# Cross attention in a six-stage layer: score matmuls as pairs of float32r tiles of 64 rows, small work cut into single matmuls at fixed steps

## What is computed

```python
q = x @ Wq;  k, v = split(ctx @ Wkv)            # heads of 16 channels
q, k = apply_axial_rope(q, pos), apply_axial_rope(k, pos)
p = softmax(q @ k.T / sqrt(16))                 # 512 x 512 for each head
y = (p @ v) @ Wout + bout
x = layernorm(x + y)
```

## Time and profile before

| | us |
|---|---|
| median of 3 runs | 3314.42 (3313.26 to 3315.32) |
| the profiled execution | 3316.54 |
| its span, first to last instruction | 3314.8 |
| TensorE busy in the span | 2716.1 (82%) |
| VectorE busy | 1958.6 (59%) |
| ScalarE busy | 1433.1 (43%) |
| GpSimd busy | 1177.7 (36%) |
| mean granted TensorE clock | 0.900 |
| exponentials of the cross attention, first to last unit | 2490.0 to 3117.5 |

### The profile page before, as it was taken

The page is one execution under the profiler, slowest core; times in us unless marked ns, Lnnn a source line. Parts: engine busy times, 40 slices in busy tenths (PEclk is TensorE's granted clock), DMA queues, the critical chain, the costliest instruction groups (busy, mean ns, idle before and its releaser), DMA issues.

```text
span 3314.8 us, 50665 instructions
## 1 busy us (share of the span) xinstructions
PE 2716.1 (82%) x20138; PEld 1454.0 (44%) x20154; DVE 1958.6 (59%) x3064; ACT 1433.1 (43%) x2577; POOL 1177.7 (36%) x1118
## 2 busy tenths in 40 slices
PE   5788888876677676589988898888768989899787
PEld 3565656553223232268845444444433333333244
DVE  3323232333689889956526566656655657476477
ACT  3232333320545555423426262635315546465555
POOL 0443333441566666600023625243243424241000
PEclk8888888887888888799998999998879989899999
DMA  2222222130330304032332424243155435252301
GB/s 87 71 59 62 52 78 60 47 87 14 121 116 13 127 26 140 13 140 95 137 108 86 128 90 125 93 122 130 39 117 107 105 69 112 61 109 53 118 26 39
DMA packets 209370, 280.04 MB, mean 84 GB/s; under 512 B 84640, under 2 KB 111680, under 8 KB 208240
## 3 DMA queue, kind: packets, MB, share of 16 engines
q1 hardware_dynamic: 209136, 276.81, 29.4%
HBM read 192.08 MB, written 59.12 MB: 76 GB/s over the span
## 4 chain that ended last, share of the span: by engine, by line
PE 39%; DVE 10%; issue 5%; ACT 4%; POOL 2%; DMA 1%; SPq 0%; ACTq 0%; DVEq 0%; POOLq 0%
PE ps L236 7%; PE ps L3368 4%; PE ps L1846 4%; PE ps L1857 4%; PE ps L3355 4%; PE ps L3341 3%; PE ps L3300 3%; PE ps L3332 2%; PE ps L2512 1%; ACT arena L3446 1%; PE ps L2520 1%; DVE arena L2775 1%; DVE arena L1434 1%; DMA arena<-arena 1%; DVE arena L2773 1%
## 5 line engine op out<-in xcount | busy, mean ns | idle before, releaser
L236 PE MATMUL ps<-arena 128*128 128x512 f32 (+3 forms) x1280 | 473.6, 522 | 18.3 <-ACT arena L2612 6.1
L3545 DVE TENSOR_REDUCE arena<-ps 128x1 f32<-128x512 f32 x512 | 330.3, 685 | 229.2 <-PE ps L3341 227.8
L3446 ACT ACTIVATE arena<-ps 128x512 f32<-128x512 f32 x512 | 287.8, 597 | 283.2 <-PE ps L3355 279.7
L1466 POOL TENSOR_TENSOR arena<-arena 128x1024 f32<-128x1024 f32 x128 | 311.0, 2430 | 192.9 <-DVE arena L1458 192.9
L1482 PE MATMUL ps<-arena 128*128 128x512 f32 x512 | 267.2, 662 | 55.8 <-POOL arena L1466 55.5
L1458 DVE TENSOR_TENSOR_SCAN arena<-ps,arena 128x1024 f32<-128x1024 f32 x128 | 291.5, 2278 | 32.9 <-ACT ps L1449 32.9
L236 PEld LDWEIGHTS ps<-arena 128*128 128x128 f32 (+2 forms) x1296 | 193.2, 154 | 252.3 <-issue 172.9
L1449 ACT ACTIVATE ps<-arena 128x511 f32<-128x511 f32 x256 | 165.1, 679 | 188.3 <-DVE arena L1458 188.1
L576 POOL TENSOR_TENSOR arena<-arena 128x31 f32<-128x31 f32 (+15 forms) x217 | 130.1, 600 | 324.2 <-DMA arena<-d_a 307.8
L3355 PE MATMUL ps<-arena 99*128 99x512 bf16 x512 | 198.4, 390 | 45.3 <-ACT arena L3446 33.4
L3341 PE MATMUL ps<-arena 96*128 96x512 bf16 x512 | 201.4, 395 | 19.1 <-issue 15.4
(11 more groups left out here) (352 smaller groups left out, 5254.1 us busy)
## 6 DMA issues: line engine op xcount, KB each, us to landing
arena<-d_bc SPq DMA_DIRECT2D x32, 1024.0 KB, 5.7
arena<-d_x SPq DMA_DIRECT2D x24, 1024.0 KB, 6.8
arena<-d_parts SPq DMA_DIRECT2D x192, 128.0 KB, 4.6
d_x<-arena SPq DMA_DIRECT2D x64, 256.0 KB, 2.5
arena<-arena SPq DMA_DIRECT2D x128, 128.0 KB, 2.1
arena<-in_D_wlm SPq DMA_DIRECT2D x12, 1024.0 KB, 6.6
d_parts<-arena SPq DMA_DIRECT2D x32, 384.0 KB, 2.4
d_signs<-arena SPq DMA_DIRECT2D x32, 256.0 KB, 2.1
```

The costliest lines, as they stand in the source:

```text
L236: ins = pe.e.matmul(ps[:m, :n], lhsT(k), rhs(k), start=(k == 0), stop=(k == chunks - 1))
L1466: pool.e.tensor_tensor(h, h, s.bc[:, turn % s.SLOTS, 1], ALU.mult).then_inc(*pool.up("scan_hC"))
L3446: act.e.activation(s.E[:, k % 2, j], s.rexp.bank((u, i)), ACT.Exp).then_inc(*s.rexp.empty(act, (u, i)))
L3545: dve.e.tensor_reduce(s.mx[:, u % 2, t, h:h + 1], s.rmax.bank((u, m)), AX.X, ALU.max, negate=True).then_inc(*s.rmax.empty(dve, (u, m)))
```

## The change

- **Scores.** q and k are split into two float32r parts (hi, lo) instead of three bf16 ones. Three products of parts give 48 rows, and two rows of ones against the two parts of the negated maximum make 50. Head 2h stands in rows 0 to 49 and head 2h+1 in rows 64 to 113, so two heads' score matmuls use the two halves of the array. A step now has two score tiles of each kind; there are 16 steps (`PAIRS`) in an iteration.
- **Small work.** `small` replaces `misc`. It gives each matmul (or group of transposes) of an item a step of its own: Rq at 3, 3, 5, 5, Rk at 7, 7, V at 9, 9 (four matmuls each time), a y tile at 11, 11, 13, 13. The y tiles of a batch spread over the next three iterations. ang and the xT stay in iterations with i a multiple of 4, at steps 11 to 15.
- **Banks.** 3 for exponential scores, 3 for maximum scores, 1 for values, 1 for small work.
- **Buffers.** `aT` has two copies. The residual of odd batches uses the buffer of x. Bias sums, residual loads, square root, scaling and stores move by some steps.
- **Queues.** A row copy is 2 transfers instead of 3; a stack stays at 6. SP first writes two rows of ones for each half. The maxima are transposed in fp32 instead of bf16.

```diff
-    Q_PARTS = (0, 1, 0, 2, 1, 0)
-    K_PARTS = (0, 0, 1, 0, 1, 2)
-    N = 6 * 16
+    Q_PARTS = (0, 0, 1)
+    K_PARTS = (0, 1, 0)
+    N = 3 * 16
     UNITS, HU = 4 * B, 8
     G = 4
     KEYS = L // P
     STEPS = HU * T
+    PAIRS = STEPS // 2
+    RESIDUAL_AT = (4, 8, 12, 13)
...
-        s.Qs, s.Ks = carve(s.SLOTS, s.HU, L, dt=BF16), carve(s.SLOTS, s.HU, L, dt=BF16)
+        s.Qs, s.Ks = carve(s.SLOTS, s.HU // 2, L, dt=F32R), carve(s.SLOTS, s.HU // 2, L, dt=F32R)
...
-        s.ring = Ring("cross", ps, 6, 2, [(name, s.EMPTIES[name[0]]) for i in s.iterations() for _, name in s.misc(i)])
-        s.rexp = Ring("cross_exp", ps, 0, 2, [((u, e), "act") for u in range(s.UNITS) for e in range(s.STEPS)])
-        s.rmax = Ring("cross_max", ps, 2, 3, [((u, m), "dve") for u in range(s.UNITS) for m in range(s.STEPS)])
-        s.rav = Ring("cross_av", ps, 5, 1, [((u, g), "act") for u in range(s.UNITS) for g in range(2)])
+        s.rexp = Ring("cross_exp", ps, 0, 3, [((u, e), "act") for u in range(s.UNITS) for e in range(s.STEPS)])
+        s.rmax = Ring("cross_max", ps, 3, 3, [((u, m), "dve") for u in range(s.UNITS) for m in range(s.STEPS)])
+        s.rav = Ring("cross_av", ps, 6, 1, [((u, g), "act") for u in range(s.UNITS) for g in range(2)])
+        s.misc = [item for i in s.iterations() for item in s.small(i)]
+        s.ring = Ring("cross", ps, 7, 1, [(name, s.EMPTIES[name[0]]) for name, _ in s.misc])
...
+    def small(self, i):
+
+        s = self
+        f, nb, b = i + s.AHEAD, (i + s.AHEAD + 1) // C, i // C - 1
         starts = (i + s.AHEAD + 1) % C == 0 and nb < B
+        items = []
+        if s.unit(i) is not None:
+            items.append((("mT", i, 1), [1]))
+        if s.unit(i - 1) is not None:
+            items.append((("turn", i - 1, 1), [2]))
         if s.unit(f) is not None and i != -1:
-            yield 1, ("Rq", f)
+            items.append((("Rq", f), [3, 3, 5, 5]))
+        if s.unit(i - 1) is not None:
+            items.append((("aT", i - 1), [6]))
+        if s.unit(f) is not None and i != -1:
+            items.append((("Rk", f), [7, 7]))
+        if s.unit(i + 1) is not None:
+            items.append((("mT", i + 1, 0), [8]))
+        if s.unit(f) is not None:
+            items.append((("V", f), [9, 9]))
         if s.unit(i) is not None:
-            yield 3, ("mT", i, 1)
-        if s.unit(i - 1) is not None:
-            yield 5, ("turn", i - 1, 1)
-        if s.unit(f) is not None and i != -1:
-            yield 7, ("Rk", f)
-        if s.unit(i - 1) is not None:
-            yield 11, ("aT", i - 1)
-        if s.unit(f) is not None:
-            yield 15, ("V", f)
-        ends = s.unit(i - 1) is not None and i % C == 0
+            items.append((("turn", i, 0), [10]))
+        if i == -2:
+            items += [(("Rq", f + 1), [11, 11, 13, 13]), (("Rk", f + 1), [15, 15])]
         if starts:
-            yield 17, ("ang", nb)
-        if s.unit(i + 1) is not None:
-            yield 19, ("mT", i + 1, 0)
-        if s.unit(i) is not None:
-            yield 21, ("turn", i, 0)
-        if i == -2:
-            yield 25, ("Rq", f + 1)
-            yield 27, ("Rk", f + 1)
-        for t in range(T):
-            if ends:
-                yield 22 + 2 * t, ("y", i // C - 1, t)
-            if starts:
-                yield 23 + 2 * t, ("xT", nb, t)
-
-
+            items += [(("ang", nb), [11])] + [(("xT", nb, t), [12 + t]) for t in range(T)]
+        if i == s.UNITS:
+            items += [(("y", b, t), [7 + 2 * t] * C) for t in range(T)]
+        elif b >= 0 and i % C:
+            items.append((("y", b, (0, 0, 2, 3)[i % C]), [11, 11, 13, 13]))
+            if i % C == 1:
+                items.append((("y", b, 1), [14, 15, 15, 16]))
+        return [(name, [s.PAIRS * i + at for at in steps]) for name, steps in items]
+
+    def pieces(self, step):
+
+        return [(name, k, len(steps)) for name, steps in self.misc for k, at in enumerate(steps) if at == step]
+
+    def ended(self, step):
+
+        return [name for name, steps in self.misc if steps[-1] == step]
+
+    def res(self, b):
+
+        return (self.xr, self.x)[b % 2]
...
-        for a in range(3):
-            sp.e.dma_start(s.Qs[96 + a:97 + a, u % s.SLOTS, s.G * half:s.G * (half + 1)],
-                           s.mT[s.G * a:s.G * (a + 1), half, :]).then_inc(*sp.up(f"cross_max_rows{half}", 16))
+        for p in range(2):
+            at = 64 * p + s.N
+            sp.e.dma_start(s.Qs[at:at + 2, u % s.SLOTS, 2 * half:2 * half + 2].bitcast(F32),
+                           s.mT[4 * p:4 * p + 4, half, :].bitcast(F32)).then_inc(*sp.up(f"cross_max_rows{half}", 16))
...
-            sp.e.dma_start(dst[16 * a:16 * a + 16], d[:, :, part, :].rearrange("h d l -> d h l")).then_inc(*sp.up(f"cross_stack_{'qk'[w]}", 16))
+            for p in range(2):
+                at = 64 * p + 16 * a
+                sp.e.dma_start(dst[at:at + 16].bitcast(F32), d[p::2, :, part, :].rearrange("h d l -> d h l")).then_inc(*sp.up(f"cross_stack_{'qk'[w]}", 16))
...
+    def sp_one_rows(self, sp):
+
+        s = self
+        sp.e.wait_ge(*sp.at_all("cross_ones"))
+        for p in range(2):
+            at = 64 * p + s.N
+            sp.e.dma_start(s.Ks[at:at + 2].rearrange("p a h l -> p (a h) l").bitcast(F32), spread(s.one[:2], 1, s.SLOTS * s.HU // 2)).then_inc(*sp.up("cross_one_rows", 16))
...
-            if i >= 0 and i % C == 0 and nb < B:
+            if i % C == 0 and nb < B:
                 s.sp_x(sp, nb)
+            if s.unit(i) is not None:
+                s.sp_rows(sp, i, 1)
+            if i % C == 0 and i >= 2 * C:
+                s.sp_store(sp, i // C - 2)
             if s.unit(f) is not None:
                 s.sp_swap(sp, f, 0)
-            if s.unit(i) is not None:
-                s.sp_rows(sp, i, 1)
-            if s.unit(f) is not None:
                 s.sp_swap(sp, f, 1)
-            if i % C == 1 and i > C:
-                s.sp_store(sp, i // C - 1)
-            if s.unit(f) is not None:
                 s.sp_stack(sp, f, 0)
             if s.unit(i + 1) is not None:
                 s.sp_rows(sp, i + 1, 0)
             if s.unit(f) is not None:
                 s.sp_stack(sp, f, 1)
-            if i >= 0 and i % C == 0 and nb < B:
+            if i % C == 0 and nb < B:
                 s.sp_ctx(sp, nb)
-            if i > 0 and i % C == 2:
-                s.sp_residual(sp, i // C)
+            if i in s.RESIDUAL_AT:
+                s.sp_residual(sp, s.RESIDUAL_AT.index(i))
...
-        hi, mid, lo = (s.parts[:, w, a] for a in range(3))
+        hi, lo = (s.parts[:, w, a] for a in range(2))
         e.tensor_copy(hi, s.m1[:, w]).then_inc(*eng.up_step("cross"))
         eng.e.wait_ge(*eng.at_step("cross"))
-        e.tensor_tensor(s.rest[:, w], s.m1[:, w], hi, ALU.subtract).then_inc(*eng.up_step("cross"))
-        eng.e.wait_ge(*eng.at_step("cross"))
-        e.tensor_copy(mid, s.rest[:, w]).then_inc(*eng.up_step("cross"))
-        eng.e.wait_ge(*eng.at_step("cross"))
-        e.tensor_tensor(lo, s.rest[:, w], mid, ALU.subtract).then_inc(*eng.up(f"cross_parts_{n}"))
+        e.tensor_tensor(lo, s.m1[:, w], hi.bitcast(F32), ALU.subtract).then_inc(*eng.up(f"cross_parts_{n}"))
...
+            ins = e.matmul(ps, wt[:, piece, cols], src[:, piece, :], start=(piece == 0), stop=(piece == pieces - 1))
...
+            for t in (2 * piece, 2 * piece + 1):
...
-                ins = e.transpose(ps.bitcast(BF16)[:3 * s.G, t * P:(t + 1) * P], s.mp[:, half, t].rearrange("p a h -> p (a h)"), s.identb)
+                ins = e.transpose(ps[:2 * s.G, t * P:(t + 1) * P], s.mp[:, name[2], t].rearrange("q p a h -> q (p a h)").bitcast(F32), s.ident)
...
-        s, slot, h, t = self, u % self.SLOTS, m // T, m % T
+        s, slot = self, u % self.SLOTS
+        hh, t, p = m // (2 * T), m // 2 % T, m % 2
...
-        pe.e.matmul(s.rmax.bank((u, m)), s.Qs[:s.N, slot, h, t * P:(t + 1) * P], s.Ks[:s.N, slot, h, :],
+        rows = slice(64 * p, 64 * p + s.N)
+        pe.e.matmul(s.rmax.bank((u, m)), s.Qs[rows, slot, hh, t * P:(t + 1) * P], s.Ks[rows, slot, hh, :],
...
-        pe.e.matmul(s.rexp.bank((u, i)), s.Ks[:s.N + 3, slot, s.G * g + j, k * P:(k + 1) * P], s.Qs[:s.N + 3, slot, s.G * g + j, :],
+        hh, p = 2 * g + j // 2, j % 2
+        rows = slice(64 * p, 64 * p + s.N + 2)
+        pe.e.matmul(s.rexp.bank((u, i)), s.Ks[rows, slot, hh, k * P:(k + 1) * P], s.Qs[rows, slot, hh, :],
...
     def pe_all(self, pe):
         s = self
         for i in s.iterations():
-            misc = dict(s.misc(i))
-            for m in range(s.STEPS):
+            for step in range(s.PAIRS):
+                tiles = (2 * step, 2 * step + 1)
                 if s.unit(i) is not None:
-                    s.pe_exp(pe, i, m)
+                    for e in tiles:
+                        s.pe_exp(pe, i, e)
                 if s.unit(i + 1) is not None:
-                    s.pe_max(pe, i + 1, m)
-                if m % s.G == 1:
```

(53 more changed lines are left out.)

165 lines of the change are left out of this document (75 added, 90 removed).

## The result

The changed kernel takes **3261.19 us** (median of 4 runs, 3251.65 to 3267.0) against 3314.8 us of the kernel before on the same chip (4 runs, 3313.26 to 3315.32): ratio 0.9836, 95% interval 0.981 to 0.9862. It is faster by 1.6%. The forecast was 3236; the range, 3190 to 3290, holds the result. The profiled execution took 3264.53 us with a span of 3262.7, 52.1 less than before; the forecast was 78 less.

The account below looks back on a forecast made before the run. TensorE was taken to set the pace. Units 78 us less (549), prologue -4, tail +4 and Ternary 0 sum to -78, giving 3236 us; range 3190 to 3290.

Parts of the forecast that it names:

- Part 1: Score matmuls on TensorE: a float32r pair in two halves costs 0.24 us, a step 0.48 instead of 0.87.
- Part 2: Changes of tile form between scores and other TensorE work: about 0.2 us in and 0.2 out, thirty changes a unit.
- fourth rival: Changes of tile form cost 0.1 us, not 0.2: 2.5 less a unit, 3196 us in all; chance 0.10.
- Part 3: Small work at fixed steps: steps sum to 31.0 us, plain unit 31.8 with waits; all units 549, 78 less.
- the last four: Last four units of the stage: 34.8 us, then without new fronts 30.5, 27 and 25.
- The prologue term: Prologue ahead of the units: four shorter rotations save 7 us, the single bank gives back 3: -4.
- Tail and Ternary: After the units: four y tiles in one bank wait for VectorE, +4 us; Ternary's later loads stay covered, 0.
- Halves that don't overlap: Score pairs: each step costs 0.46 us more on TensorE, 88 in all, 3324 us; chance 0.07.
- Late maximum rows: Maximum rows landing 3 us later cost 2 in most units, 25 in all: 3261 us; chance 0.12.
- A lower clock: Granted clock falls in the units; at 0.84 they last 40.8 us, 105 more in all: 3341; chance 0.05.
- Doesn't add up: Small work and scores: ScalarE and VectorE stall each other, every unit at 39 us, no change, 3314; chance 0.02.

Follow-up runs that it names:

- experiment 2: Changed kernel with both tiles of each score pair in the same half of the array, the next pair in the other: 3340.86 us, ratio 1.007.
- experiment 1: The changed kernel itself run again, nothing altered, as base for other runs: 3267.32 us, ratio to before 0.9873.
- experiment 6: Changed kernel with banks 4 exponential, 2 maximum, 1 values, 1 small work instead of 3, 3, 1, 1: 3286.28 us, ratio 0.9925.
- experiment 8: Changed kernel with SyncE issuing the next stack's copy to DRAM ahead of this stack's six loads in the prologue: 3251.13 us, ratio 0.9827.
- experiment 5: Changed kernel with banks 2 exponential, 3 maximum, 1 values, 2 small work instead of 3, 3, 1, 1: 3248.99 us, ratio 0.9807.
- experiment 7: Changed kernel with the last batch's four y tiles in the three banks of the maxima instead of the single small-work bank: 3249.16 us, ratio 0.9829.

## Why the prediction was right, and where it was not

**Part 1, a pair at 0.24: right.** 0.24 between pairs of one form; experiment 2 gives the price without overlap, 73 to 76 us where the rival had 88, and 3341 in all where it had 3324. By the Trainium skill's 3.07 of 4 ("TensorE: Matmul & The Clock Gate") a pair would be 0.31 (0.235 x 4/3.07, an estimate; the prediction has 0.30); the trace says 0.24 for this form, two tiles of 64 rows, which that table doesn't list.

**Part 2, changes at 0.2 in and 0.2 out: too dear for transposes, right for projections.** Entering transposes costs 0.12 (0.36 from pair to transposes, 2600.85 to 2601.21, instead of 0.24). Leaving costs 0.09 (four transposes at 0.11 would be 0.44, the next pair starts 0.53 behind), and the pair behind a change another 0.1 (0.34). That is 0.31 a round trip, not 0.4. Around a query piece it is 0.39: 0.33 from pair to first matmul (0.09, 2609.12 to 2609.45), 1.92 to the next pair where two matmuls are 1.72 (0.20, half of it in the first matmul, half behind the last), and again 0.1 behind that pair. So the cheaper changes of the fourth rival hold for one kind of block only. The Trainium skill ("TensorEngine Tiling (Array Packing)", key properties) says that a change of mode drains TensorE; no single part reaches the 0.16 that the forecast took for a full drain, so the rows don't show one.

**Part 3, the plain unit: right, 31.8 against 31.5 to 33.3** (i = 1 to 3; 31.5 to 32.4 in experiment 1), and step by step in i = 2, from an odd step's scores to the next odd step's:

| steps | 1,2 | 3,4 | 5,6 | 7,8 | 9,10 | 11,12 | 13,14 |
|---|---|---|---|---|---|---|---|
| forecast | 3.6 | 4.24 | 4.88 | 4.88 | 4.95 | 2.8 | 2.8 |
| measured | 3.75 | 4.52 | 4.84 | 4.93 | 4.98 | 2.94 | 2.94 |

The forecast's steps hold no waits; it charged 0.8 for them beside the sum. Measured, the steps stand 0.9 above the sum: 0.4 at the three floors (2.94 instead of 2.8), the rest in steps 1 to 4, where TensorE waits for the values' bank and the small bank (0.24 us ahead of 2605.23 for VectorE). So the unit came out because a floor taken too low and bank waits charged too high offset each other. Units 0 to 11 sum to 432.3 against 431.8: i = 4, 5, 6, 8 at 37.3, 37.0, 35.5 and 41.0 (forecast 39, 38.3, 34.7, 42).

**The step that failed in the units is the last four**, "34.8, then without new fronts 30.5, 27, 25": 36.4, 33.4, 29.9, 28.9, 11.3 us more, nearly the whole miss of the stage. (The first read a clock of 0.91 here; in experiment 1 it read 0.95 and took 34.6. The other three are the same there within 0.1.) The floor was taken as the larger of chain and TensorE's sum. But the chain from scores through exponentials to values passes through TensorE, so small work behind the values adds to it: in the last unit two empty steps take 2.67, and with four transposes behind the values 3.25. A second term was left at nothing: twice a unit ScalarE copies the values' bank out between exponentials, and the next values block waits for it, which makes the 3.16 and 3.15 of experiment 6:

```profile
3042.12 1.06 PE L3401 MATMUL ps<-cross,cross 128*32 128x512 f32 x8 [0.48 <-ACT cross L3490]
```

Where the new projections vanish, most steps stand at chain plus such work (i = 14: 2.93 for two empty steps, 3.52 with transposes). The mechanism of the floor was right in the last unit (experiment 6): 0.53 to the first exponential, two of 0.52, 0.10 to release, then the values, 2.67 where the forecast had 2.8. In units with maxima the waits stand elsewhere, as shown there, and the 2.94 is not settled by a run.

**The prologue term failed in both its parts**: "four shorter rotations save 7, the single bank gives back 3: -4". Measured +3.9 in the first profile. Shorter rotations bring 2 to 3 us (75.9 before, 72.8 and 73.9 with two banks; none at all with one, 80.1 against 79.4 to 81.3), because four of the five on GpSimd were not on the path: each was done 7 us or more before its copy was issued (2466.90 against 2474.06 before). The cadence of the stacks is SyncE's own chain: two swap issues, the landing of the copy to DRAM behind the previous stack's transfers, six load issues. The 10.0 of the prediction was the last interval; the four average 9.8 before and 9.7 after. The copy's growth costs nothing there: from issue to the first load it is 5.9 before with 384 KB,

```profile
2465.37 0.58 SPq L3166 DMA_DIRECT2D d_parts<-arena  x1
```

to 2471.28 in the earlier trace rows, and 5.7 after with 512 KB (2460.28 to 2465.96 in experiment 8). Only the first copy, with no loads ahead of it, went from 2.3 to 2.9. Only the first rotation is on the path, and with two banks alone: 10.0 us before (2429.76 to 2439.73), 8.0 in experiment 5 (2435.43 to 2443.39). With one bank SyncE is still busy with later swaps when it ends (2441.20, first copy at 2443.86). And the single bank costs 4 to 8 (80.1 against 75.9 with bf16 scores, 79.8 and 81.3 against 72.8 and 73.9), since each of four x transposes and each projection waits 0.69 to 0.78 for ScalarE in a stretch that has nothing else to do:

```profile
2418.78 1.08 PE L3314 MATMUL ps<-cross,cross 128*128 128x128 f32 x4 [3.21 <-ACT cross L3447]
2420.55 1.12 PE L3314 MATMUL ps<-cross,cross 128*128 128x128 f32 x4 [0.69 <-ACT cross L3442]
...
2432.90 1.96 PE L3320 MATMUL ps<-cross,cross 128*128 128x512 f32 x4 [0.78 <-ACT cross L3454]
```

**Tail and Ternary, +4 and 0: came out at +11.4** in the first profile, and 5.1 to 11.4 in the eight profiles with one bank and no remedy. The single bank is 3 of it (4.48 instead of 3.44 from tile to tile, three times), close to the 4 that was charged. The rest appears beside a lower granted clock: the first y tile takes 6.73 where the next take 3.70, and 5.15 in experiment 2's run; Ternary takes 178.0 us at a clock of 0.94 before, 182.9 at 0.89 after, and 178.4 at 0.95 in experiment 7. No run holds the clock fixed, and none shows why it was lower, so this part stays open.

**Rivals.** Halves that don't overlap: refuted. Late maximum rows: one unit begins with a wait of 1.31 us for them,

```profile
2631.42 0.50 PE L3388 MATMUL ps<-cross,cross 50*128 50x512 f32 x2 [1.31 <-DMA cross<-cross]
```

(i = 4), one with 0.17 (i = 2), and that is all behind the first unit: 1.5 us, not 25. A lower clock: plain units read 0.96 to 1.00. "Doesn't add up": the two halves of the change sum to 74 us alone and give 67 to 69 together.

**What was luck.** The measured 3261 is, to the microsecond, the total of the rival with late maximum rows, whose waits did not come. The forecast was 25 us too low, from the last four units, the prologue, and tail and Ternary; its range had room for them, but was made wide for other reasons.

## What to carry to other kernels

Price a faster matmul by what stands between: here the halved scores alone brought 0.6%, and spreading a crowd of output tiles over other units, with the banks that go with it, 1.1%. Before you price a shorter instruction in a chain of transfers, look whether the chain waits for it: four of five shorter rotations here saved nothing. When a chain passes through the engine you are counting, don't take the larger of chain and sum; work queued behind the chain's link adds to it. Buffers given to the steady state are missing at both ends of a stage, where others lie idle: lend those.

## What the runs showed of the hardware

- Two float32r matmuls of 48 or 50 rows and 128 columns in the two 64-row halves cost what one costs: 0.24 us for 512 columns each; in one half the second starts 0.23 behind the first, 0.47 for both (experiment 2).
- A pair that follows another tile form takes 0.34 us to the next pair instead of 0.24, even from exponential to maximum scores of the same form. I had priced only the first start, not this second one; what causes it was not tested.
- A write to DRAM issued behind six loads of the same queue took 5.5 to 5.9 us to land (the last of the prologue 7.1 to 7.2), with 384 KB as with 512; with no loads ahead of it 2.3 and 2.9. Issued ahead of the loads it left the path, and the prologue lost 8 to 10 us (experiment 8).
- The same code ahead of the stage took 2407 to 2425 us in the profiles of the changed kernel and its variants. The changed kernel's times spread over 15 and 21 us in its two series, those of the kernel before over 2 us in the first series and 12 to 22 in four later ones; so a difference under 10 us is read from the same stretch in two profiles, not from two totals.
